# A language-model tower on one core: router logits taken from widened matmuls, and the softmax of the second attention handed over in smaller pieces

## The reference, cut to what matters

```
h  = h + attn1(layernorm(h))              # 12 heads of 16, rotary q and k, softmax, w_proj, b_proj
xf = layernorm(h)
router_probs = softmax(xf @ router_w)     # 8 experts
expert_index = argmax(router_probs)       # a token goes to one expert, with a position by cumsum
                                          # and dropped beyond the expert's capacity (512)
out = gelu(gelu(expert_inputs @ w1 + b1) @ w2 + b2), scaled by the gate
```

## Time and profile before

| | |
|---|---|
| median of 3 runs | 1372.17 us (1368.9 to 1372.8) |
| the profiled execution: its own time | 1371.76 us |
| its span | 1370.1 us |
| mean granted clock of PE | 0.986 of full speed |
| combine_phase, about | 852 to 1227 us of the span |
| PE, DVE, ACT, POOL busy over the whole span | 96%, 71%, 69%, 18% |

### The profile page before, as it was taken

How to read it: one execution, slowest core, us unless ns; L and a number is a source line. 1 busy time by engine, 2 the same in 40 slices (tenths; PEclk the granted TensorE clock), 3 DMA queues, 4 the chain that set the end, 5 groups by cost and what they waited for, 6 DMA issues and landing times.

```text
span 1370.1 us, 29508 instructions
## 1 busy us (share of the span) xinstructions
PE 1309.8 (96%) x8890; PEld 1169.0 (85%) x8890; DVE 976.6 (71%) x2984; ACT 948.7 (69%) x2360; POOL 252.3 (18%) x284
## 2 busy tenths in 40 slices
PE   8789999999999999999999999899999999979997
PEld 6578888888889988998899898788888889868986
DVE  7988888557787777777777774588888888732341
ACT  1478888888766666666666664488888888835552
POOL 5332110000111111111111110012122122121335
PEclk9999999999999999999999999999999999988999
DMA  7144444457666666666666666444554547115542
GB/s 204 43 151 162 157 160 150 154 191 236 196 203 188 204 189 200 191 203 188 203 194 199 191 186 214 139 151 145 155 163 142 150 143 219 33 36 141 129 98 23
DMA packets 179747, 219.99 MB, mean 161 GB/s; under 512 B 23460, under 2 KB 146570, under 8 KB 179648
## 3 DMA queue, kind: packets, MB, share of 16 engines
q1 hardware_dynamic: 146256, 178.61, 42.6%
q10 hardware_dynamic: 25712, 33.19, 7.3%
q0 software_dynamic: 7680, 6.95, 2.6%
HBM read 141.31 MB, written 79.90 MB: 161 GB/s over the span
## 4 chain that ended last, share of the span: by engine, by line
PE 60%; ACT 8%; DVE 3%; issue 2%; DMA 1%; POOL 0%; POOLq 0%; SPq 0%; ACTq 0%; DVEq 0%
PE bank L115 25%; PE bank L1354 22%; ACT probs L1853 5%; PE bank L1729 3%; PE bank L1766 2%; PE bank L91 2%; DVE head_neg_max L1963 1%; PE bank L94 1%; PE bank L1774 1%; ACT probsT L1872 1%; PE bank L1808 1%; PE bank L1828 1%; PE bank L1751 1%; ACT headsT_kq L1877 1%; PE bank L122 1%
## 5 line engine op out<-in xcount | busy, mean ns | idle before, releaser
L1354 PE MATMUL bank<-e_w,e_h_full 128*128 128x192 f32 x1920 | 324.9, 326 | 0.4
L1354 PEld LDWEIGHTS bank<-e_w,e_h_full 128*128 128x128 f32 x1920 | 310.6, 190 | 1.7 <-ACT e_h_full L1435 1.3
L1435 ACT ACTIVATE e_h_full<-bank,e_b 128x512 f32<-128x512 f32 x240 | 165.2, 689 | 155.5 <-PE bank L115 155.4
L1290 POOL TENSOR_TENSOR e_ln_rstd<-e_ln_var_eps,minus_half 128x4 f32<-128x4 f32 x62 | 62.4, 1006 | 437.1 <-DVE e_ln_var_eps L1486 437.1
L1853 ACT ACTIVATE probs<-bank,head_neg_max 128x128 f32<-128x128 f32 x384 | 134.6, 391 | 7.8 <-DVE head_neg_max L1963 5.8
L1493 DVE TENSOR_SCALAR e_rows<-e_slot_sums,e_ln_mean_var,e_ln_rstd 128x192 f32<-128x192 f32 x248 | 77.5, 376 | 77.5 <-POOL e_ln_rstd L1290 77.5
L1396 ACT ACTIVATE e_x_full<-bank,e_ln_shift,e_ln_gain 128x512 f32<-128x512 f32 x124 | 76.5, 667 | 40.7 <-issue 36.7
L1103 PE MATMUL bank<-x,dispatch_weights 128*128 128x193 f32 x512 | 95.9, 329 | 5.6 <-ACT slot_stage L948 4.8
L115 PE MATMUL bank<-e_x_hi,e_w1hi 128*128 128x512 f32 x216 | 95.5, 442 | 2.5 <-PEq L551 1.4
L1729 PE MATMUL bank<-slot_outputs_then_w_part,combineT 128*128 128x193 f32 x512 | 94.3, 337 | 2.4 <-ACT combineT L1845 2.1
L1729 PEld LDWEIGHTS bank<-slot_outputs_then_w_part,combineT 128*128 128x128 f32 x512 | 84.8, 192 | 8.9 <-issue 8.2
(11 more groups left out here) (290 smaller groups left out, 3100.3 us busy)
## 6 DMA issues: line engine op xcount, KB each, us to landing
slot_sums<-slot_stage SPq DMA_DIRECT2D x64, 386.0 KB, 3.2
e_slot_sums<-slot_sums SPq DMA_DIRECT2D x64, 386.0 KB, 3.6
slot_outputs<-e_stage ACTq DMA_DIRECT2D x64, 384.0 KB, 3.6
slot_outputs_then_w_part<-slot_outputs SPq DMA_DIRECT2D x30, 768.0 KB, 4.9
e_w<-in_w SPq DMA_DIRECT2D x64, 288.0 KB, 3.0
slot_logits<-kept_logits SPq DMA_DIRECT2D x32, 512.0 KB, 3.0
slot_logits<-slot_logits SPq DMA_DIRECT2D x32, 512.0 KB, 3.4
e_w1raw<-in_w SPq DMA_DIRECT2D x80, 192.0 KB, 2.7
```

What stands on the lines that cost most here:

```text
L1290: pool.tensor_tensor(rs[u][:], ve[u][:], half[:], ALU.pow).then_inc(rstd_ready, 1)
L1354: last = pe.matmul(y, hf[:, k, js], w2s[u][:, k, :], start=k == 0, stop=k == MT - 1)
L1435: act.activation(hf[:, m, :], hbank(u, m), act_fn, bias=b1s[:, m, ds(n, 1)]).then_inc(acted, 1)
```

## The change

It has five parts. The names r, z, w, p and so on are those of the pipeline above.

1. Router logits. Because layernorm is linear up to its scale, the logits are split: the router matrix, centred over its rows, is put behind the v columns of the weights (192 to 200 columns), and its product with `w_proj` and `b_proj` behind the projection's columns (192 to 200). ACT scales the 8 extra v columns by the standard deviation (`ln4_std`, a second power on POOL) into 8 extra columns of `h_all`, and the residual add then adds the projection's 8. The logits' exponential takes the second layernorm's scale. The transposes L1751, the copy `x5T` and the router matmuls go. Preparing the centred matrix and the product adds a few instructions in the first two turns, and five DMAs.
2. The pipeline is a turn shorter: r, z and w come one turn earlier.
3. The transposes of the probabilities wait for the exponentials by thirds (`4 * a + 2 + k`).
4. Maxima: one per bank (four instead of two), at the end of the turn behind `x4T_hi_over_lo` and ahead of `x_rows`, no longer at the start of the next turn behind `x_rows`.
5. Moves: values by head are copied on ACT one turn later, behind the exponentials; the reciprocals are turned over ahead of the scores, in bank 3; the rotary sum goes ahead of the residual on DVE; PE computes Y of batch 1 in turn 0; `keep_busy(10)` in turns 0 and 1 becomes 6 matmuls inside Y of batch 0 and 3 in turn 1; POOL's two scatters stand on either side of the powers.

```diff
         sp.dma_start(self.sin[:], ins["sin"]).then_inc(self.tables_in, 16)
-        sp.dma_start(self.Wp[:], ins["Wproj"]).then_inc(self.tables_in, 16)
+        sp.dma_start(self.Wp[:, :, 0:D], ins["Wproj"]).then_inc(self.tables_in, 16)
+        sp.dma_start(self.WpT[:, 0, :], ins["WprojT"][0:P]).then_inc(self.WpT_in, 16)
+        sp.dma_start(self.WpT[0:DR, 1, :], ins["WprojT"][P:D]).then_inc(self.WpT_in, 16)
+        for c, rows, of in ((0, slice(0, P), slice(0, P)), (1, slice(0, DR), slice(P, D)), (1, slice(DR, P), slice(P, D))):
+            sp.dma_start(self.R[rows, c, :], ins["router"][of]).then_inc(self.R_in, 16)
         sp.dma_start(self.rank[:], ins["rank"].partition_broadcast(P)).then_inc(self.router_in, 16)
         sp.dma_start(self.numbers[:], ins["numbers"]).then_inc(self.router_in, 16)
...
-            for t in range(NB + 6):
+            for t in range(NB + 5):
                 turn(t, t % 2, batch(t + 1), batch(t), batch(t - 1), batch(t - 2), batch(t - 3),
-                     pair(5, t), pair(6, t), pair(7, t))
...
-            past(eng, S["counts_read"], r if r is not None else z)
...
+                        scatter(w, 0)
                     if y is not None:
-                        rsqrt(0, y)
+                        powers4(y)
                     if p is not None:
-                        rsqrt(1, p)
+                        rsqrt5(p)
+                    if w is not None:
+                        scatter(w, 1)
...
+                def sum_router():
+                    pe.wait_ge(early.R_in, 48)
+                    pe.wait_ge(S["ones_table"], 1)
+                    matmuls(pe, R_sums, [(ones[:], early.R[:, 0, :]), (ones[0:DR], early.R[0:DR, 1, :])]
+                            ).then_inc(S["R_summed"], 1)
+
+                def project_router():
+                    pe.wait_ge(early.WpT_in, 32)
+                    pe.wait_ge(S["R_centred"], 1)
+                    for g in range(2):
+                        gs = slice(g * P, (g + 1) * P)
+                        last = matmuls(pe, WpR[:, g, :], [(early.WpT[:, 0, gs], Rc[:, 0, :]),
+                                                          (early.WpT[0:DR, 1, gs], Rc[0:DR, 1, :])])
+                    last.then_inc(S["WpR_done"], 1)
+
+                def outputs_of(y, u):
...
+                            pe.wait_ge(early.ys_last_in[u], 16)
+                        last = pe.matmul(bank[:, 0, 0:D + 1], cT[:, c, :], ysb[u][:, c, :],
+                                         start=c == 0, stop=c == NC - 1)
+                    last.then_inc(S["Y_done"], 1)
+
                 def heads_of(o, c, done):
...
+                            outputs_of(0, 0)
+                            sum_router()
+                            outputs_of(1, 1)
+                        elif y > 1:
+                            outputs_of(y, u)
...
+                            project_router()
...
-                    if r is not None:
-                        bank7_free(pe, a, r, z)
-                        pe.wait_ge(S["x5_ready"], 2 * r + 2)
-                        for j in range(2):
-                            for k in range(2):
-                                last = pe.transpose(bank[:, 7, (2 * j + k) * P:(2 * j + k + 1) * P],
-                                                    x5[r % 3][:, j, TAG + k * DR:TAG + k * DR + P], ident[:])
-                        last.then_inc(S["x5T_done"], 1)
                     if z is not None:
-                        bank7_free(pe, a, r, z)
+                        pe.wait_ge(S["S_exp"], 4 * (NB if a is None else a + 1))
...
                     if a is not None:
-                        pe.wait_ge(S["S_exp"], 4 * a + 4)
                         for k in range(3):
+                            pe.wait_ge(S["S_exp"], 4 * a + 2 + k)
...
-                    if r is not None:
-                        if r == 0:
-                            pe.wait_ge(router_in, 64)
-                        pe.wait_ge(S["x5T_took"], r + 1)
-                        for j in range(2):
-                            last = matmuls(pe, bank[:, 7, j * P:(j + 1) * P],
-                                           [(x5T[:, j, 0, :], rw0[:]), (x5T[:, j, 1, :], rw1[:])])
-                        last.then_inc(S["router_done"], 1)
-                    if t < 2:
-                        keep_busy(pe, T, bank[:, 6, :], 10)
+                    if t == 1:
+                        keep_busy(pe, T, bank[:, 6, :], 3)
...
-                        heads_of(bank[:, 3, 0:D], slice(2 * D, 3 * D), "v_done")
+                        if q == 0:
+                            pe.wait_ge(S["R_split"], 1)
+                            pe.wait_ge(S["WpR_took"], 1)
+                        heads_of(bank[:, 3, 0:D + NE1], slice(2 * D, 3 * D + NE1), "v_done")
+                    if a is not None:
+                        past(pe, S["v_took"], min(a + 1, NB))
+                        past(pe, S["einvT_took"], a)
+                        pe.wait_ge(S["einv_ready"], a + 1)
+                        for g in range(2):
+                            last = pe.transpose(bank[:, 3, (2 + g) * P:(3 + g) * P], einv_wide[:, g, :], ident[:])
+                        last.then_inc(S["einvT_done"], 1)
+                    if q is not None:
                         pe.wait_ge(S["qk_took"], q + 1)
                         if a is not None:
...
-                        if r is not None:
-                            pe.wait_ge(S["logits_read"], r + 1)
...
-                        pe.wait_ge(S["einv_ready"], a + 1)
-                        for g in range(2):
-                            last = pe.transpose(bank[:, 2, g * P:(g + 1) * P], einv_wide[:, g, :], ident[:])
-                        last.then_inc(S["einvT_done"], 1)
...
+                def take_values(a, u):
+                    if a == 0:
+                        act.wait_ge(S["values_padded"], 4)
+                    act.wait_ge(S["v_done"], a + 1)
+
+                    past(act, S["head_out_done"], a - 1)
+                    act.wait_ge(S["ln4_std"], a + 1)
+                    act.activation(T["h_wide"][:, a, D:], bank[:, 3, D:D + NE1], ACT.Copy,
+                                   scale=std4[:, a % 4:a % 4 + 1])
+                    by_halves = vs[u][:].rearrange("p (i b) (e d) -> p i (b e) d", b=2, e=2)
+                    act.activation(by_halves[:, :, 0:4:3, :],
+                                   bank[:, 3, 0:D].rearrange("p (i b d) -> p i b d", b=2, d=HD), ACT.Copy
+                                   ).then_inc(S["v_took"], 1)
+
...
                         for s in range(4):
-                            act.wait_ge(S["head_max"], 2 * a + s // 2 + 1)
+                            act.wait_ge(S["head_max"], 4 * a + s + 1)
...
-                    if r is not None:
-                        act.wait_ge(S["x5T_done"], r + 1)
-
-                        past(act, S["router_done"], r)
-                        act.activation(x5T[:].rearrange("p j k t -> p (j k t)"), bank[:, 7, :], ACT.Copy
-                                       ).then_inc(S["x5T_took"], 1)
+                        take_values(a, u)
                     if z is not None:
                         act.wait_ge(S["logits_read"], z + 1)
-                        act.activation(lex[:], lx[:], ACT.Exp).then_inc(S["router_exped"], 1)
+                        act.wait_ge(S["ln5_rstd"], 2 * z + 2)
+                        past(act, S["lex_summed"], z)
+                        for j in range(2):
+                            c = (2 * z + j) % 4
+                            last = act.activation(lex[:, j, :], lx[:, j, :], ACT.Exp, scale=rs5[:, c:c + 1])
+                        last.then_inc(S["router_exped"], 1)
...
-                    if q is not None:
-                        if q == 0:
-                            act.wait_ge(S["values_padded"], 4)
-                        act.wait_ge(S["v_done"], q + 1)
-
-                        past(act, S["head_out_done"], q - 1)
-                        by_halves = vs[1 - u][:].rearrange("p (i b) (e d) -> p i (b e) d", b=2, e=2)
-                        act.activation(by_halves[:, :, 0:4:3, :],
-                                       bank[:, 3, 0:D].rearrange("p (i b d) -> p i b d", b=2, d=HD), ACT.Copy).then_inc(S["v_took"], 1)
...
-                    dve.wait_ge(S["router_done"], r + 1)
+                    dve.wait_ge(S["h3_ready"], 2 * r + 2)
                     past(dve, S["router_exped"], r)
...
+                    logits = T["h_wide"][:, 2 * r:2 * r + 2, D:]
+                    st.link(dve.tensor_reduce(nlm[:], logits, AX_X, ALU.max, negate=True))
+                    dve.tensor_tensor(lx[:], logits, nlm[:].unsqueeze(2).broadcast_to([P, 2, NE1]), ALU.add
                                       ).then_inc(S["logits_read"], 1)
...
-                    if a is not None:
-                        past(dve, S["S_exp"], 4 * a)
-                        for k in range(2):
-                            dve.wait_ge(S["S_done"], 4 * a + 2 * k + 2)
```

(18 more changed lines are left out.)

148 lines of the change are left out of this document (89 added, 59 removed).

## The result

The changed kernel takes 1355.92 us (median of 4 runs, 1355.16 to 1358.08) against 1371.83 us of the kernel before (1368.9 to 1372.8): on record as a ratio of 0.990, 95% interval 0.988 to 0.992. (The two medians divide to 0.988, 15.9 us; 0.990 would be 13.7 us.) The sign was right and the median lies in the range of 1330 to 1358, near its upper end; the gain is about half of the one forecast.

What follows compares the result with a forecast made beforehand. DVE's loop and the chain over PE were taken to bound the steady turn at 9.8 us: 27 × (10.47 − 9.8) = 18.1, start 3.0 + 1.1, end 6.4, together 28.6 us off 1371.8, so 1343 us; range 1330 to 1358.

Steps and rivals of the forecast that it cites:

- A dead heat: Steady turn: DVE's loop of 9.74 us and the chain over PE of 9.78 tie, so 9.8 a turn.
- PE alone: Steady turns: PE alone decides and DVE's loop shrinks, turns of 9.5 us, 1335 us in all; chance 0.20.
- PE's work: Steady turns: PE's work falls to 9.26 us in a routed turn and, without waits, 9.76 in a counting one.
- DVE's loop, term by term: Steady turn on DVE, maxima round to maxima, waits left out: 9.55 us, with 0.19 for four maxima 9.74.
- The rotary sum ahead of the residual, "worth 0": On DVE: both still stand before x, and q and k's transposes wait for the residual anyway, so worth 0.
- The order of `x_rows` and the maxima doesn't change the loop.: DVE's loop, behind `x4T_hi_over_lo`: putting the maxima ahead of `x_rows` leaves its length unchanged.
- POOL's order: POOL: one more power a batch, but x needs only the first, and POOL is busy for 57.73 of 282.66 us.
- Four maxima: DVE's loop: four of 384 take 2.0 us, 0.19 more than two; the skill's fixed cost gave 0.25.
- The hand-overs rival: Steady turns: three near-equal loops over three engines leave no slack, 10.1 us a turn, 1353 us; chance 0.22.
- The start: To the first maximum: 3.0 us less, bounds 0 and 5, from fewer spare matmuls and Y of batch 1 moved.
- The ends: End of the phase: turn 32 falls by 1.6 us, turn 33 to the last scatter by 4.8.
- The clock: Slower rival: PE's pauses before x's transposes drop its clock; about 1385 us with a third of turns; chance 0.03.

Runs made afterwards that it cites:

- e5: Changed kernel with the combine logits' maximum subtracted for only one chunk of eight in batches 5 to 30, for timing only: 1350.7 us, ratio 0.985.
- e8: Changed kernel with the residual ahead of the rotary sum, `x_rows` ahead of the maxima and the second scatter behind the turn's first maximum: 1341.8 us, 0.979.
- e2: Changed kernel with the residual again ahead of the rotary sum on DVE: 1347.8 us, 0.985.
- e3: Changed kernel with `x_rows` again ahead of the four maxima on DVE, maxima still at the turn's end: 1350.0 us, 0.987.
- e7: Changed kernel with the pair's second scatter on POOL issued only when the turn's first maximum is ready: 1352.2 us, 0.986.
- e11: Changed kernel with two maxima of 768 in place of four of 384, exponentials waiting for their pair: 1356.9 us, 0.990.
- e4: Changed kernel with the five added loads (router, Wproj's transpose) issued right behind the Wqkv loads: 1357.7 us, 0.993.
- e9: The e8 kernel with the five added loads also issued early, behind the Wqkv loads: 1343.7 us, 0.981.
- e12: The e8 kernel with all table loads of the second attention issued right behind the Wqkv loads: 1345.2 us, 0.981.
- e1: Changed kernel with both scatters of a pair again one behind the other, ahead of the powers on POOL: 1362.3 us, 0.9955.
- e13: Kernel before with Wproj in a tile 8 columns wider; no total given, store landed after 3.4 us, first maximum at 875.45.

## Why the prediction was half right

- *What bounds it.* "A dead heat" of DVE's loop and PE's chain was the right picture, and e5 confirms how near they are. The rival "PE alone" didn't hold in the changed kernel; e8's counting turns are of that kind.
- *PE's work.* Right: 9.76 us for a counting turn forecast, 9.72 in e8's chain (1018.56 to 1028.28). For routed turns 9.26 was about right as work (e8's 9.73 less 0.3 of idle time and 0.2 of slower transposes), but PE waits for the rotary sum and the residual there; that wait was forecast for x.
- *DVE's loop, term by term* (routed and counting turn, rows above; the forecast in brackets): maxima to `rope_straight` 4.52 and 4.40 (4.46), `rope_straight` to x 3.24 in both (3.06), x to `x4T_hi_over_lo` 1.76 in both (1.68), from there to the maxima 0.88 and 0.46 (0.54). The mean is 10.13 where the forecast has 9.74: the second term misses 0.18, the third 0.08, and the last 0.13, although `x_rows` (0.28) no longer stands in it. The first came out right by luck: `x_rows` now stands there and wasn't counted, and other pieces of the term were shorter than forecast.
- *The rotary sum ahead of the residual, "worth 0".* The failed step: +0.19 us a turn, 5 us in all (e2). The sum took `rope_straight` to x as 3.06 in an order in which it is 3.24.
- *"The order of `x_rows` and the maxima doesn't change the loop."* Also failed: 0.15 us a turn, 4 us (e3). With `x_rows` behind them the maxima don't start earlier, since they wait for the scores.
- *POOL's order.* The prediction only asked when the powers come. It left out what the second scatter meets: the scores' late semaphore, 0.42 us in every second turn by the rows. e7 got back 0.10 a turn of it; the other half went into the longer `x_rows`.
- *Four maxima.* Forecast 2.0 us against 1.81 for two; measured 1.95 (1016.72), 0.14 more than two. From start to the next instruction's start it is 1.87 against 1.73 in e11. So 0.19 was a little and the 0.25 set beside it much too high, and e11 shows that the earlier exponentials pay for it. ScalarE: forecast 8.9 us of work a turn, measured 238.56 / 27 = 8.84.
- *The hand-overs rival* had 0.22 and priced 10.1 us a turn: the measured turn. Its reasons (`headsT_kq`, reciprocals, the first third) were not the ones. That the time lies in the stated range rests on this case, whose number came true without its mechanism: luck.
- *The start.* Forecast −3.0. From the issue of the first outputs' load that waits for the store, to the first maximum, the changed kernel needs 19.8 and 18.5 us in two profiles, the kernel before 21.7 and 19.8, 1.6 less on average; the store's landing takes 1.8 back. "The five DMAs are hidden" was right by e4, e9 and e12, though not for the start as a whole.
- *Turns 2 to 4.* 9.45 each forecast, 9.80 measured. PE's idle times of 1.04 and 0.20 us for the exponentials went, but it then idled 0.79, 0.48 and 0.49 us for the rotary sum or the residual, as in the steady turns.
- *The ends.* 1.7 and 3.9 against 1.6 and 4.8.
- *The clock.* 1.00 in the steady stretch, with PE's pauses of 0.55 us in it. In the 12 us at the start it was 0.64 and 0.72 in the two profiles of the changed kernel, 0.72 and 0.86 in those of the kernel before.

Two of the three harmful edits were stated in the prediction as neutral, with no row that showed it; with the 0.19 and 0.15 that e2 and e3 measured, 9.8 becomes 10.1 a turn. The third, the place of the second scatter, wasn't in the sum at all. And the 9.8 itself was reached: by the version without the three, at 1341.8 us.

## What to carry to other kernels

Where two loops over different engines come out equal, as here, look at the order of the small instructions inside them and not only at the work taken out: put an independent instruction (here `x_rows`) wherever the loop waits for a neighbour, and keep a producer a few instructions ahead of the instruction that reads it. After such a change read the timeline of one turn of each kind and ask of each idle gap what could stand in it; the two exchanges and the held scatter brought 13.7 us here, nearly as much as the change. And to learn which engine decides, take some work off it: of 0.9 us a turn off DVE, 0.15 came back before the three edits and nothing after them.

## What the runs showed of the hardware

- The scores' semaphore is late when POOL starts an indirect DMA just ahead of them. With the matmul that sets it issued 0.62 to 0.65 us behind the start of the scatter, it was set 0.65 to 0.70 us behind the matmul's start in place of 0.28, in 13 of 13 turns of the changed kernel; with the scatter 1.7 to 1.8 us behind that matmul (e7) or over 4 us ahead of it (e1) it was 0.28 in all steady turns. That the scatter is the cause is shown by these two runs; by which mechanism is not.
- A DVE instruction that starts 0.5 us behind such a scatter can be longer too: `x_rows` took 0.59 us in place of 0.37 in 12 of 13 turns of e7. That it is the scatter is argued from its place alone; no run moved it again with nothing else.
- Four maxima of 384 fp32 elements from PSUM take 1.87 us from the first's start to the next instruction's (0.47 each), two of 768 take 1.73 (e11): here splitting costs 0.14 us, 0.07 for each instruction more.
- The last store of the small experts' outputs (384 KB) landed 4.3 to 5.4 us behind its issue in every trace of the changed kernel and its variants, and 2.9 to 3.4 us behind it in those of the kernel before and e13; what delays it is not found.
